# Two-layer graph network on one core: count blocks made up to 42 quads ahead of the messages, from index tiles of their own; stores in two steps a group; two batches of visits a step afterwards

## The reference

```
# layer 0
m   = silu([x[src], x[dst], edge] @ mW1 + mb1) @ mW2 + mb2
agg = segment_sum(m, dst)
y   = layernorm(x + silu([x, agg] @ uW1 + ub1) @ uW2 + ub2) * gamma + beta
x1  = layernorm(x + y)
# layer 1
agg1 = segment_sum(x1[src], dst) / max(deg, 1)
out  = layernorm(x1 + relu(relu([x1, agg1] @ W1 + b1) @ W2 + b2))
```

## Time and profile before

| | |
|---|---|
| median of 3 runs | 2902.84 us (2895.51 to 2920.19) |
| profiled execution | 2885.56 us, its span 2883.7 us |
| busy PE / DVE / ACT / POOL | 2275.3 / 1681.2 / 1475.2 / 1518.6 us |
| granted TensorE clock, mean | 0.817 |
| first and last silu of a quad start at | 85.7 us / 2747.6 us |

### The profile page before, as it was taken

How to read it: one execution, slowest core, us unless ns; L and a number is a source line. 1 busy time by engine, 2 the same in 40 slices (tenths; PEclk the granted TensorE clock), 3 DMA queues, 4 the chain that set the end, 5 groups by cost and what they waited for, 6 DMA issues and landing times.

```text
span 2883.7 us, 58406 instructions
## 1 busy us (share of the span) xinstructions
PE 2275.3 (79%) x19559; PEld 1944.8 (67%) x19559; DVE 1681.2 (58%) x5671; ACT 1475.2 (51%) x3771; POOL 1518.6 (53%) x1633
## 2 busy tenths in 40 slices
PE   5778777878787888777777778878888788887986
PEld 4666666666676766666666667767677676776874
DVE  5465655665555565565565656566555556555735
ACT  3454554555464554454555555455555454554614
POOL 5555556556555555555555555455554555554322
PEclk7776777877777876887888888888888888898998
DMA  6454555554555564555565555666565666666683
GB/s 218 121 153 142 148 152 152 160 150 150 162 155 154 153 175 142 177 166 169 152 182 164 174 173 176 185 167 182 165 187 173 174 193 173 186 173 192 200 296 97
DMA packets 305361, 487.72 MB, mean 169 GB/s; under 512 B 121342, under 2 KB 183944, under 8 KB 305056
## 3 DMA queue, kind: packets, MB, share of 16 engines
q10 hardware_dynamic: 94161, 245.05, 26.0%
q1 hardware_dynamic: 158895, 129.93, 16.4%
q0 software_dynamic: 52000, 108.96, 14.4%
HBM read 375.62 MB, written 108.13 MB: 168 GB/s over the span
## 4 chain that ended last, share of the span: by engine, by line
PE 48%; another core or an unknown queue 15%; issue 14%; DVE 10%; ACT 9%; ACTq 3%; DMA 1%; DVEq 0%; SPq 0%
PE ps_pre L1200 12%; PE ps_cnt L1221 11%; PE ps_l L1257 9%; PE ps_sum L1241 8%; DVE edgeK L966 4%; ACT counts L1363 3%; PE ps_pre L1207 3%; ACT farN L1399 2%; DVE edgeL L964 2%; ACT h L1419 1%; ACTq L1496 1%; PE ps_sum L1243 1%; DVE pre L979 1%; DVE nodeE L956 1%
## 5 line engine op out<-in xcount | busy, mean ns | idle before, releaser
L899 POOL DMA_INDIRECT gath<-P_d,src_i x1527 | 1444.3, 946 | 1185.4 <-DVE pre L979 748.0
L1200 PE MATMUL ps_pre<-wc,eT_c 128*128 128x128 f32 x3128 | 730.2, 354 | 61.7 <-issue 59.7
L1221 PE MATMUL ps_cnt<-edgeK,edgeL 128*128 128x250 bf16 (+1 forms) x3128 | 578.0, 338 | 197.8 <-ACT counts L1363 110.1
L1200 PEld LDWEIGHTS ps_pre<-wc,eT_c 128*128 128x128 f32 x3128 | 593.3, 234 | 119.6 <-issue 84.5
L966 DVE TENSOR_SCALAR edgeK<-iotaK,key 128x500 bf16<-128x500 f16 (+1 forms) x1564 | 667.7, 488 | 0.0
L979 DVE TENSOR_TENSOR pre<-ps_pre,gath 128x512 f32<-128x512 f32 x384 | 262.9, 685 | 686.5 <-remote 462.9
L1363 ACT ACTIVATE counts<-ps_cnt 128x1000 bf16<-128x1000 f32 x391 | 405.5, 1037 | 414.9 <-remote 228.2
L1241 PE MATMUL ps_sum<-edgeN,h 128*128 128x40 f32 x3128 | 481.5, 302 | 80.6 <-issue 68.9
L1221 PEld LDWEIGHTS ps_cnt<-edgeK,edgeL 128*128 128x128 bf16 x3128 | 319.0, 111 | 309.9 <-issue 210.3
L1241 PEld LDWEIGHTS ps_sum<-edgeN,h 128*128 128x128 f32 x3128 | 448.7, 217 | 101.2 <-issue 79.8
L1257 PE MATMUL ps_l<-A_v,x1h 128*128 128x120 bf16 x5020 | 359.7, 229 | 85.6 <-issue 74.6
(11 more groups left out here) (184 smaller groups left out, 1425.0 us busy)
## 6 DMA issues: line engine op xcount, KB each, us to landing
eT_c<-eT ACTq DMA_DIRECT2D x193, 512.0 KB
A_d<-counts ACTq DMA_DIRECT2D x168, 384.0 KB
rel_c<-rel_d ACTq DMA_DIRECT2D x193, 240.0 KB
A_v<-A_d SPq DMA_DIRECT2D x68, 448.0 KB
A_v<-A_d SPq DMA_DIRECT2D x97, 256.0 KB
gath<-P_d,src_i POOLq DMA_INDIRECT x1535
A_d<-counts ACTq DMA_DIRECT2D x56, 416.0 KB
A_v<-A_d SPq DMA_DIRECT2D x33, 384.0 KB
```

Of the source, the lines that this page charges most:

```text
L899: pool.indirect_dma_start(gath[:, r, t * D:(t + 1) * D], None, v["P_d"], bass.IndirectOffsetOnAxis(ap=src_i[g % RS][:, c:c + 1], axis=0)). ...
L1200: T.matmul(o, eT_c[c % RE][:, e0:e0 + P], wc[:], start=True, stop=False)
L1221: last = T.matmul(o[:, :, w0:w0 + w], edgeL[x][:, j, 0:P], r, start=(j == 0), stop=(j == QT - 1 and q == 0), skip_group_check=True)
```

## The change

Counts are taken out of the messages' step. `plan_counts` gives each count a step of its own: one a step as before, and from step 12 on a second one at every sixth step (42 of them: 12, 18, ..., 258), so that counts run up to 42 quads ahead. The last count is made in step 347, and steps 348 to 390 have none. PE makes the extra count between the visits and sums(s), the main one behind sums(s) as before; ACT, at a step with an extra one, copies the previous main count before silu(s) and the extra one behind it. The keys come from index tiles of their own (`src_c`, `dst_c`, `first_c`, 3 more small SP loads a group, L765 being the old ones), `make_keys` follows the counts, and what is left of it for the messages is `relate`. The stores of a group go 2 and 2, in the steps in which the first two counts of the next group are copied. From step 355 (`COUNTED + LEAD`) to 391 a step may have two batches of visits of at most 14 blocks in 3 visits each, one before and one behind sums(s), down to 2 blocks a visit; and all 12 slots are open from there on. Worked out from the planner: visits are the same, at the same steps, up to step 355; then 622 blocks instead of 518 lie in steps 348 to 391 (172 visits instead of 69), and 352 instead of 456 behind, in 27 batches loaded by 27 transfers instead of 34 batches by 65. The first final unit is at step 409 in both, the last visits at step 419 instead of 425. 528 visits instead of 443 hold the same blocks. In number the matmuls, the counts, the copies and the gathers stay as they were.

```diff
+EARLY, EVERY, FIRST_EXTRA = 42, 6, 12
+def plan_counts():
+    main, extra, c, s = {}, {}, 1, 0
+    while c < NQ:
+        if s >= FIRST_EXTRA and s % EVERY == 0 and c - s - 1 < EARLY:
+            extra[s], c = c, c + 1
+        if c < NQ:
+            main[s], c = c, c + 1
+        s += 1
+    copied = {0: 0, **{c: s + 1 for s, c in main.items()}, **{c: s for s, c in extra.items()}}
+    stores = {}
+    for c in range(GQ, NQ):
+        if 1 <= c % GQ <= len(PARTS) // 2:
+            stores.setdefault(copied[c], []).extend((c // GQ - 1, 2 * (c % GQ - 1) + k) for k in range(2))
...
 def plan_visits(units):
+        s, second = divmod(t, 2)
+        if second and not COUNTED + LEAD <= s < QUADS:
+            t += 1
+            continue
...
-        for _ in range(2 if s < QUADS else 4):
+        for _ in range(2 if s < COUNTED + LEAD else 3 if s < QUADS else 4):
...
-                if s < (d + 1) * GQ + GQ + 2 or zeroed < NB and ...
+                if s < STORED[d] + LEAD + 1 or zeroed < NB and ...
...
 # SP
+        def load_count_ids(g):
+            k = g % 2
+            if g >= 2:
+                sp.wait_ge(keyed, g - 1)
+            sp.dma_start(src_c[k][:], v["src_pt"][:, g * GT:(g + 1) * GT]).then_inc(c_in[k], 16)
+            sp.dma_start(dst_c[k][:], v["dst_pt"][:, g * GT:(g + 1) * GT]).then_inc(c_in[k], 16)
+            sp.dma_start(first_c[k][:], v["dst_first"][g * GT:(g + 1) * GT].partition_broadcast(P)).then_inc(c_in[k], 16)
...
+                for c in range(GQ + 1, NQ, GQ):
+                    if COUNT_STEP[c] == s and c // GQ + 1 < GROUPS:
+                        load_count_ids(c // GQ + 1)
...
 # DVE, step s
-                if s + 1 < NQ:
-                    if q == GQ - 1:
-                        dve.wait_ge(prepared, g + 2)
-                    hots(s + 1)
-                if s - 1 in VISITS_AT:
-                    add_visits(s - 1)
+                for c in (COUNT_AT.get(s), EXTRA_AT.get(s + 1)):
+                    if c is not None:
+                        if c % GQ == 0:
+                            dve.wait_ge(prepared, c // GQ + 1)
+                        hots(c)
+                        if c % GQ == 3 and c // GQ + 1 < GROUPS:
+                            make_keys(c // GQ + 1)
+                        if c % GQ == GQ - 1:
+                            clear(c // GQ + 1)
+                for t in ADDED_EARLY.get(s, ()):
+                    add_visits(t)
...
+                if s in ADDED_LATE:
+                    add_visits(ADDED_LATE[s])
...
 # PE, step s, behind products(s+1) and the unit's step
-                for i in VISITS_AT.get(s, ()):
+                for i in VISITS_AT.get(2 * s, ()):
                     visit(i)
...
+                if s in EXTRA_AT:
+                    count(EXTRA_AT[s])
                 if s < NQ:
                     sums(s)
-                if s + 1 < NQ:
-                    count(s + 1)
+                for i in VISITS_AT.get(2 * s + 1, ()):
+                    visit(i)
+                if s in COUNT_AT:
+                    count(COUNT_AT[s])
...
 # ACT, step s
+                made = 0 if s == 0 else COUNT_AT.get(s - 1)
+                if s + 1 < NQ:
+                    distances(s + 1)
+                if s in EXTRA_AT:
+                    copy_next(made)
                 if s < NQ:
                     activate(s)
                     load_chunk_of(s)
...
+                if s in EXTRA_AT:
+                    copy_next(EXTRA_AT[s])
+                elif made is not None:
+                    copy_next(made)
+                for g, part in STORES_AT.get(s, ()):
+                    store(g, part)
```

More of the change, by code:

```diff
@@ L80, in plan_units @@
     return units + [(LAST_B, NB, QUADS)]
+def plan_counts():
[11 more added lines that the diff above has]
+            stores.setdefault(copied[c], []).extend((c // GQ - 1, 2 * (c % GQ - 1) + k) for k in range(2))
+    for part in range(len(PARTS)):
+        stores.setdefault(copied[NQ - 1] + 1 + part // 2, []).append((GROUPS - 1, part))
+    stored = {g: s for s in sorted(stores) for g, part in stores[s] if part == len(PARTS) - 1}
+    return main, extra, stores, stored
+COUNT_AT, EXTRA_AT, STORES_AT, STORED = plan_counts()
+COUNT_STEP = {0: 0, **{c: s for s, c in COUNT_AT.items()}, **{c: s - 1 for s, c in EXTRA_AT.items()}}
+COUNTED = max(STORES_AT) + 1
 def plan_visits(units):
-    done, visits, s = [0] * GROUPS, [], 0
+    done, visits, t = [0] * GROUPS, [], 0
     while sum(done) < GROUPS * NB:
+        s, second = divmod(t, 2)
+        if second and not COUNTED + LEAD <= s < QUADS:
+            t += 1
+            continue
         ready = max([hi for lo, hi, s0 in units if s0 + U_LEN <= s], default=0)
@@ L122, in plan_last @@
         start[s] = now
-        blocks = sum(VISITS[i][3] - VISITS[i][2] for i in VISITS_AT.get(s, ()))
-        now += max(0.1 * blocks, 0.3 * len(VISITS_AT.get(s, ())), 1.5 if s <= QUADS + U_LEN else 0.7)
+        blocks = sum(VISITS[i][3] - VISITS[i][2] for i in VISITS_AT.get(2 * s, ()))
+        now += max(0.1 * blocks, 0.3 * len(VISITS_AT.get(2 * s, ())), 1.5 if s <= QUADS + U_LEN else 0.7)
     steps, first = [], 0
     for w in range(len(LAST_UNITS)):
-        first = max(first, start[VISITS[LAST_VISIT[w]][0] + 1] + 2)
+        first = max(first, start[VISITS[LAST_VISIT[w]][0] // 2 + 1] + 2)
         steps += [(next(s for s in start if start[s] >= first + t), first + t, w, k) for k, t in enumerate(L_STEPS)]
@@ L203, in changes_of_sums @@
             at["zero", UNIT_AT[s][0]] = n
+        for i in VISITS_AT[ADDED_LATE[s]] if s in ADDED_LATE else ():
+            n += 1
+            at["visit", i] = n
     return at
@@ L684, in build_edges @@
     first_i = [v["first_i0"], sb("first_i1", [P, GT], I32)]
+    src_c, dst_c, first_c = ([sb(f"{n}_c{k}", [P, GT], I32) for k in range(2)] for n in ("src", "dst", "first"))
     nodeE = [sb(f"nodeE{k}", [KQ, QT * P], BF16) for k in range(2)]
@@ L719, in build_edges @@
     onehots = sem("onehots")
+    related = sem("related")
+    c_in = [sem(f"c_in{k}") for k in range(2)]
     keyed, far, near = sem("keyed"), sem("far"), sem("near")
@@ L1140, in fast @@
         def fast():
+            relate(0)
             make_keys(0)
@@ L1486, in fast, with copy_next @@
         def fast():
-            off = 0
+            offset = [0]
+            def copy_next(c):
+                ahead = 0
+                if c % GQ < GQ - 1 and c + 1 < NQ:
+                    ahead = act.value_load(offs[0:1, c + 1:c + 2], min_val=0, max_val=LASTQ)
+                copy_counts(c, offset[0], ahead)
+                offset[0] = ahead
             distances(0)
```

109 lines of the change are left out of this document (51 added, 58 removed).

## The result

| | before | changed |
|---|---|---|
| median of 4 runs | 2911.52 us (2895.51 to 2931.67) | 2973.77 us (2966.28 to 2975.93) |
| profiled execution, its span | 2885.56 us, 2883.7 us | 2974.76 us, 2973.0 us |
| granted clock, mean | 0.817 | 0.815 |

The ratio is 1.0223, 95% interval 1.0184 to 1.0262: 2.2% slower, where 2900 us was forecast, and outside the range of 2850 to 2952 us. All of this stands at one level of time, near 2900 us. Late in the study the same two kernels ran near 2130 us; the last part of the experiments is about that level, where the change is 0.8% faster. What follows here is the first level.

What follows compares the result with a forecast made beforehand. PE was taken to set the pace, late by itself, early with ACT and DVE close behind. 60 - 50 + 16 - 4 - 24 = -2 us against 2885.56 gave 2884 us, scaled to the median 2900 us; range 2850 to 2952 us.

Steps and rivals of the forecast that it cites:

- 42 extra counts: Steps 12 to 258: second counts cost +60 us, mostly PE's own time; bounds 15 and 107 us.
- Rival A: Extra steps: DVE decides, each extra count costs its full 2.55 us, 107 in place of 60 us; 2948 us, chance 0.17.
- PE released by DVE: Sign of Rival A: steps with an extra count 2.5 us longer than their neighbours, PE released by DVE.
- 43 steps without a count: Steps 348 to 390: PE waits for no copy, so the whole count is gained, -50 us; bounds -44 and -60.
- Doubled visits: Steps 355 to 391: 104 blocks more cost PE 13 us and DVE's adds 3 us, +16 us (11 to 40).
- rival D: From step 355: doubled visits wait once a late load or register read adds 0.8 us; +29 us, 2930 us, chance 0.08.
- Index tiles, stores and clears: Earlier stores free `clear` of its waits, small index loads cost nothing: -4 us for stores, 0 us for loads.
- Behind the last quad: After the last quad: 11 us less PE work and 13 us of waits gone, -24 us (bounds -11 and -32).
- What is late next: Behind the last quad: the last unit's own chain, then the final units, would be late next; no size given.
- Rival C: Granted clock follows PE's load: early clock up 0.03 saves 31 us, late steps give back 8; 2878 us, chance 0.09.
- Rival B: Early extra counts nearly free, filling waits of PE: 15 in place of 60 us; 2856 us, chance 0.24.
- Stalls held fixed: Stalls of 4 to 7 us, PE, ACT and DVE standing together, until gathers end: number assumed unchanged, cause unknown.

Runs made afterwards that it cites:

- no_extra: The changed kernel without the 42 extra counts, the rest of the change kept: 2907.73 us, 0.9996 of the kernel before.
- late_single: The changed kernel with one batch of visits a step up to step 391 and 4 slots, counts still ending at step 347: 2957.39 us, 1.0171 of before.
- late_filled: The changed kernel with 8 unused matmuls of a count's size put back in each step without a count: 2979.87 us, 1.0210 of before.
- experiment 6: The kernel before and the changed kernel, each without the gathers from quad 9 on and the wait for them: 1991.17 and 2073.99 us.
- experiment 3: Two variants of the changed kernel's late steps, late_filled (unused matmuls put back) and late_single (single batches of visits): 2979.87 and 2957.39 us.

## Why the prediction was wrong, point by point

The forecast of +60 -50 +16 -4 -24 = -2 us became +99.6, -3.1 for the second and third term together, +6 and -13.4: +89.

- **42 extra counts, "I take 60 us".** This is the step that failed: 99.6 us by the two profiles, 73 to 100 by all that run this stretch. The 60 were 55 us of PE's own time and 5 us for DVE's need above it, a sixth of 30, since stalls let DVE catch up; ACT's 2.1 us a count had no term. In the trace it is the other way round. PE's busy time grows by 21.5 us (1315.57 to 1337.10), at a clock of 0.81 against 0.79, and its idle time by 78 us, or by 43 against no_extra. What PE waits for there is ACT's copy of the last count, 69 us more than before (54 more than no_extra). Without gathers the same wait is 30.5 of 36.0 us more idle time. So the term that failed is the wait, put at 5 us and put down to DVE, where the trace has 43 to 78 us and ACT ends most of it. Why the copy is late, by two counts in one step on two one-hot buffers and one pair of banks, or by ACT's own reads, copies and stores, stays open. The sixth was a guess, and that stalls cover for DVE is not borne out.

  The rows for this reading, steps 12 to 258 of the kernel before and of the changed one (columns as in the earlier trace rows):

```profile
164.16:1826.29 1662.13, 1315.57 (x10494) 1119.31 (x10494) 982.74 (x3303) 876.21 (x2290) 934.91 (x988) 0.79 0.54 161
```

```profile
168.56:1930.29 1761.73, 1337.10 (x10883) 1136.70 (x10881) 1090.36 (x3687) 916.92 (x2366) 938.02 (x992) 0.81 0.54 158
```

  Rival A gave nearly the size (107 us for 99.6), but not the mechanism: with DVE's one-hots thin the loss was 1.66% still. The text "PE released by DVE" for A was half seen: in the trace PE is released by ACT, 185 us, while DVE waits for PE.
- **43 steps without a count, "the whole count is gained".** It failed at this level: late_single gives 25.5 us against the kernel before (steps 348 to 389: 254.7 for 280.2) where 50 were forecast, and 30 against no_extra. The last nine steps paid in full (9.5 us in late_filled, 8.9 in late_single). In the 33 ahead of them a count is worth 0.2 to 0.7 us, for the granted clock fell from 0.88 to 0.80, and to 0.76 in late_single. I divided by the clock of before, as if it stayed. Without gathers, at full clock, the term is right: 32.1 + 9.6 = 42 us.
- **Doubled visits, +16 us.** Measured +22 us (late_single against changed; 17 to 24 by the others), so the direction and the size are about right. PE's waits for loads or `sumT`, rival D's sign, are not in the trace. But the chain that D describes is: in steps 355 to 389 silu stands 108.5 us for DVE's add, 17.0 in late_single. What that costs by itself wasn't measured.

```profile
ACT h L1481 <- DVE pre L1033: 108.5, 28, 9.7
...
DVE sumT L1066 <- remote: 62.0, 11, 9.0
DVE sumT L1066 <- PE ps_l L1317: 44.7, 27, 7.9
```

- **Index tiles, stores and clears, -4 us.** 0.9996 in no_extra, whose interval of 12 us either way can't tell -4 from 0.
- **Behind the last quad, -24 us.** -13.4 us at this level, -17.7 at the other. The waits for loads went, as assumed, but the final units wait more. PE from the last silu of the changed kernel on answers to the earlier trace rows:

```profile
PE ps_cnt L1387 <- ACT pre L1530: 14.5, 9, 5.5
PE ps_sum L1301 <- ACT h L1481: 2.4, 1, 2.4
PE ps_l L1317 <- DVE sumT L1066: 1.9, 5, 0.5
```

  It was 6.4 us for the final units' copies before, so 8 of the 13 us came back there, and the clock in the first 45 us is 0.86 instead of 0.92. "What is late next" was named and not priced.
- **Rival C.** The early clock rose from 0.77 to 0.79, short of the 0.80 that was its sign, and the stretch got longer all the same, since PE was waiting more. The late clock fell, which it priced at 8 us, and that took half of the second term.
- **Rival B** (nearly free) was wrong at this level and is what happens at the other: 6.4 us for 42 counts, though for POOL's pace and not for stalls.
- **Stalls held fixed.** I couldn't say what they were. They need the gathers, and, as the same program has them in some groups of runs and not in others, something besides that no record shows. They were not fixed either: the moments in which all three engines stand add up to 90 and 126 us without extra counts and to 87 to 177 us with them (experiment 6). A part of the 73 to 100 us may be theirs; the spread is too wide to say how much.

## What to carry to other kernels

A step that gets a second piece of work of one kind meets whatever that kind has only one or two of, here one pair of banks, one engine that copies them out, and two buffers ahead of them: price these waits by writing the step out, for every engine of the chain, not only the busy time of each. Work taken out of a stretch that ran partly at half clock was worth a fraction of itself here, since the clock fell further. Look how far kernels with the same program in a stage differ in it before a difference is read. And read which engine never rests at the level at which the kernel runs: with POOL bound by its gathers, the moved counts cost next to nothing and the shorter end is most of what is left.

## What the runs showed of the hardware that I had not expected

- The same program, with the same 1527 gathers of 0.95 us, took 2878 to 2912 us (clock 0.82) in some groups of runs and 2132 to 2135 us (0.94) in others, and one chip had both. Leaving the gathers out gave 1991 us (0.97) beside 2903, and 1975 us (0.98) beside 2134. So at the slower level some 900 us come with the gathers, at the faster one 160.
- 8 matmuls a step added for nothing cost 0.2 to 0.5 us a step where the clock was half for part of the time, and 1.05 us where it was nearly full (experiment 3).
- The first silu starts 84.8 to 88.4 us after the beginning of the span in all profiles of the slower groups and at 70.3 to 71.1 us in all of the faster ones, and the kernels without gathers go with their group (85.7 and 86.3, 70.3 to 70.7), so some 15 us of the difference lie in the start.
